# A Perceiver block on one core: convolution in token layout on GpSimd, bias row on VectorE, and some reordering

## The reference

```python
x = x + xattn(layernorm(x), ctx, ctx)     # q, k, v and output projections with biases, one head, softmax over 8192 keys
x = x + linear_attn(layernorm(x))         # 16 heads of 32: relu(rmsnorm(q)), relu(rmsnorm(k)); q (k^T v) / (q sum(k) + eps), W_out, b_out
x = x + ffn(layernorm(x))
# ffn, with h = layernorm(x), 8 experts, the 2 best by sigmoid(h Wr) + router_bias:
routed = sum over e < 4 of cw[e] * ((silu(h Wg[e]) * (h Wu[e])) Wd[e])
routed += cw[4] * h + cw[6] * h + cw[7] * relu(h)
shared = depthwise causal convolution of h over tokens, 4 taps, one weight per tap and channel, + conv_b
ffn = routed + shared
```

## Time and profile before

| | us |
|---|---|
| median of 3 runs | 531.51 |
| the profiled execution | 530.95 |
| its span, first to last instruction | 529.1 |
| TensorE busy | 524.3 |
| VectorE busy | 362.2 |
| ScalarE busy | 243.7 |
| GpSimd busy | 198.4 |

### The profile page before, as it was taken

The page is one execution under the profiler, slowest core; times in us unless marked ns, Lnnn a source line. Parts: engine busy times, 40 slices in busy tenths (PEclk is TensorE's granted clock), DMA queues, the critical chain, the costliest instruction groups (busy, mean ns, idle before and its releaser), DMA issues.

```text
span 529.1 us, 6966 instructions
## 1 busy us (share of the span) xinstructions
PE 524.3 (99%) x2542; PEld 436.5 (82%) x2542; DVE 362.2 (68%) x624; ACT 243.7 (46%) x392; POOL 198.4 (38%) x130
## 2 busy tenths in 40 slices
PE   9999999999999999999999999999999999999997
PEld 8888888888888888888888888888888878988886
DVE  5573666866668776556878554999967368548747
ACT  5743434745445454444535454657455332552210
POOL 3727050331211312233144442447439939900000
PEclk9999999999999999999999999999999999999999
DMA  8811222332422233422322211243330403300002
GB/s 297 321 60 61 80 97 102 111 129 81 159 81 79 81 118 123 157 82 81 141 96 80 81 56 65 79 160 119 119 121 1 159 2 123 117 1 0 2 0 79
DMA packets 15153, 51.60 MB, mean 98 GB/s; under 512 B 1808, under 2 KB 2320, under 8 KB 14480
## 3 DMA queue, kind: packets, MB, share of 16 engines
q1 hardware_dynamic: 14976, 51.03, 27.0%
q10 hardware_dynamic: 144, 0.13, 0.1%
HBM read 50.11 MB, written 1.05 MB: 97 GB/s over the span
## 4 chain that ended last, share of the span: by engine, by line
PE 97%; DVE 1%; ACT 1%; issue 0%; POOL 0%; POOLq 0%
PE bank L1405 27%; PE bank L1520 11%; PE bank L1531 11%; PE bank L1533 11%; PE bank L1521 11%; PE bank L1522 11%; PE bank L1532 11%; PE bank L1395 1%; PE bank L1452 1%; PE bank L1416 1%; PE bank L1668 1%; PE bank L1430 1%; DVE xT_l L911 0%; PE bank L1787 0%; ACT xn L651 0%; DVE stats L895 0%
## 5 line engine op out<-in xcount | busy, mean ns | idle before, releaser
L556 POOL TENSOR_TENSOR cn_l<-raw_n,cn_h 128x1024 fp32r<-128x1024 f32 x32 | 77.7, 2427 | 197.9 <-ACT cn_h L717 197.9
L735 ACT COPY ring<-bank 128x512 f32<-128x512 f32 x64 | 37.7, 589 | 148.3 <-PE bank L1522 148.0
L1030 DVE TENSOR_TENSOR top<-top,bank 128x512 f32<-128x512 f32 x60 | 41.1, 686 | 88.5 <-ACT ring L735 88.5
L1520 PE MATMUL bank<-qk_h,ct_h 128*128 128x512 f32 x256 | 99.6, 389 | 0.0
L1522 PE MATMUL bank<-qk_h,ct_l 128*128 128x512 f32 x256 | 99.6, 389 | 0.0
L1521 PE MATMUL bank<-qk_l,ct_h 128*128 128x512 f32 x256 | 99.6, 389 | 0.0
L1531 PE MATMUL bank<-ph,cn_h 128*128 128x512 f32 x256 | 99.6, 389 | 0.0
L1532 PE MATMUL bank<-pl,cn_h 128*128 128x512 f32 x256 | 99.6, 389 | 0.0
L1533 PE MATMUL bank<-ph,cn_l 128*128 128x512 f32 x256 | 99.6, 389 | 0.0
L1533 PEld LDWEIGHTS bank<-ph,cn_l 128*128 128x128 f32 x256 | 48.1, 188 | 10.1
L1522 PEld LDWEIGHTS bank<-qk_h,ct_l 128*128 128x128 f32 x256 | 48.1, 188 | 10.0
(11 more groups left out here) (248 smaller groups left out, 855.5 us busy)
## 6 DMA issues: line engine op xcount, KB each, us to landing
raw_t<-ctx_t SPq DMA_DIRECT2D x32, 512.0 KB, 4.2
raw_n<-ctx_n SPq DMA_DIRECT2D x32, 512.0 KB, 3.3
piece_raw<-pieces SPq DMA_DIRECT2D x12, 512.0 KB, 3.3
xs<-x SPq DMA_DIRECT2D x4, 256.0 KB, 5.5
wq_raw<-wq_t SPq DMA_DIRECT2D x4, 256.0 KB, 6.2
wk_raw<-wk_in SPq DMA_DIRECT2D x1, 1024.0 KB, 8.1
w_k_raw<-wqkv_in SPq DMA_DIRECT2D x1, 1024.0 KB, 7.4
w_out_raw<-wout_in SPq DMA_DIRECT2D x1, 1024.0 KB, 5.5
```

Source lines behind the costliest of these rows:

```text
L556: pool.tensor_tensor(cn[p % CNB][1][:], raw_n[p % 2][:], cn[p % CNB][0][:].bitcast(F32), ALU.subtract).then_inc(cnl_ready, 1)
L1030: dve.tensor_tensor(top[:], top[:], bank[:, S_BANKS[i % 2], :], ALU.max).then_inc(max_done, 1)
L1520: pe.matmul(bank[:, dst, :], ct[i // 2 % 2][0][:, c, keys], qk[0][:, c, :], start=(c == 0), stop=False)
```

## The change

- Bias row. The two products on TensorE, the split of `bv_wo` and `ones_r` go. VectorE sums `bv_wo` over partitions itself: `sum_bias` (at tile 9: transposition, sum), `gather_bias` (at 11: three small copies, a sum, four small copies), `spread_bias` (at 13: transposition, addition of `bo`).
- Head. The first half of `wo` is cast by VectorE, as its first instruction. VectorE's `first_stats(3)` moves ahead of `low_xT(0)`, ScalarE's `std_of(3)` ahead of `high_xT(1)`.
- Heads. TensorE makes `linear(2)` for chunks 0 and 1 only, then transposes the first tile's heads, chunks 0 and 1 as soon as VectorE's first half is there, then the rest of `linear(2)`. The z product of each tile is written as two halves; for tile 3 `transpose_x2(1)` stands between them.
- Convolution. `xf`, `whole_xT`, VectorE's four instructions for each chunk and TensorE's transposes go. The normalised tiles are written to DRAM (`xn_rows`, with three rows of zeros ahead) and loaded back three times, 1, 2 and 3 rows shifted, into two buffers `shifted`; taps and bias are loaded as rows broadcast to all partitions (`taps`, behind piece 8). GpSimd, after its last split, makes each tile with eight instructions of 128x512. Tile 1 waits for the router's weights.
- VectorE adds convolution tiles 0 to 2 in m = 6 and tile 3 behind `low_hid(7)`; expert 2 is added ahead of `low_hid(7)`.

```diff
+                if n == 8:
+                    sp.wait_ge(kv_psum, C)
+                    sp.dma_start(taps[:], taps_in.partition_broadcast(P)).then_inc(taps_loaded, 16)
+                if n == 10:
+                    sp.wait_ge(pads_ready, 2)
+                    sp.dma_start(xn_rows[0:PAD, :], tap_term[0:PAD, :]).then_inc(rows_written, 16)
+                    write_rows(0)
+            sp.wait_ge(rows_written, 16 * 2)
+            for t in range(TT):
+                b = t % 2
+                if t == 1:
+                    for n in range(1, TT):
+                        write_rows(n)
+                    sp.wait_ge(rows_written, 16 * (TT + 1))
+                    sp.wait_ge(g_psum, IC)
+                if t >= 2:
+                    sp.wait_ge(conv_ready, t - 1)
+                for j in range(1, TAPS):
+                    at_row = PAD + t * P - j
+                    sp.dma_start(shifted[b][:, j - 1, :], xn_rows[at_row:at_row + P, :]).then_inc(shift_loaded[b], 16)
...
+            pool.wait_ge(taps_loaded, 16)
+            for t in range(TT):
+                pool.wait_ge(xn_ready, 2 * TT + t + 1)
+                if t == 1:
+                    pool.wait_ge(cw_ready, 1)
+                conv_chain(pool.tensor_tensor(conv[:, t, :], xn[:, t, :], taps[:, PAD, :], ALU.mult))
+                conv_chain(pool.tensor_tensor(conv[:, t, :], conv[:, t, :], taps[:, TAPS, :], ALU.add))
+                pool.wait_ge(shift_loaded[t % 2], 16 * PAD * (t // 2 + 1))
+                for j in range(1, TAPS):
+                    conv_chain(pool.tensor_tensor(tap_term[:], shifted[t % 2][:, j - 1, :], taps[:, PAD - j, :], ALU.mult))
+                    ins = pool.tensor_tensor(conv[:, t, :], conv[:, t, :], tap_term[:], ALU.add)
+                    if j < PAD:
+                        conv_chain(ins)
+                ins.then_inc(conv_ready, 1)
...
+            dve.wait_ge(wo0_loaded[0], 16)
+            dve.tensor_copy(wo[0][:, 0, 0:HALF], wo_raw[:, 0, 0:HALF]).then_inc(wo0_ready, 1)
...
+            first_stats(3)
             low_xT(0, XT_BANKS)
-            first_stats(3)
...
+                if m == M - 2:
+                    for t in range(TT - 1):
+                        add_conv(t)
+            add_expert(EM - 2)
             low_hid(M - 1)
-            add_expert(EM - 2)
-            for t in range(TT):
-                dve.wait_ge(conv_psum, t + 1)
-                add_term(t, bank[:, t, :], None)
+            add_conv(TT - 1)
...
-                    pe.matmul(bank[:, BV_BANK, :], some, bv_parts[0][:], start=True, stop=False)
-                    pe.matmul(bank[:, BV_BANK, :], some, bv_parts[1][:], start=False, stop=True).then_inc(bv_psum, 1)
...
             transpose_heads(0)
+            linear(2, (2, 3))
             linear(TT - 1)
...
-            for t in range(TT):
-                for c in range(C):
-                    ins = pe.transpose(bank[:, t, c * P:(c + 1) * P], conv[:, c, t * P:(t + 1) * P], ident[:])
-                ins.then_inc(conv_psum, 1)
             down(M - 2)
             down(M - 1)
```

More of the change, by code:

```diff
@@ L368, in perceiver_block @@
         down_psum = sem("down_psum")
-        conv_psum = sem("conv_psum")
+        taps_loaded = sem("taps_loaded")
+        rows_written = sem("rows_written")
+        shift_loaded = [sem(f"shift_loaded{b}") for b in range(2)]
         out_ready = sem("out_ready")
@@ L692, in _ @@
             apply_of(2)
+            std_of(3)
             high_xT(1, XT_BANKS)
-            std_of(3)
             apply_of(3)
@@ L1661, in _, with linear @@
                         ins.then_inc(kv_psum, 1)
-            def linear(t):
+            def linear(t, chunks=range(C)):
                 pe.wait_ge(qrT_ready, C)
-                for c in range(C):
+                for c in chunks:
                     if t == 0:
@@ L1669, in linear @@
                                     qrT[:, c, t * P:(t + 1) * P], kv[:, c, :], start=True, stop=True)
-                ins.then_inc(la_psum, 1)
-            for t in range(TT - 1):
-                linear(t)
-            def transpose_heads(t):
-                pe.wait_ge(heads_ready, t + 1)
-                transpose_tile(heads, t, HEAD_BANKS[t]).then_inc(xnT_psum, 1)
+                if c == C - 1:
+                    ins.then_inc(la_psum, 1)
+            linear(0)
+            linear(1)
+            linear(2, (0, 1))
+            def transpose_heads(t):
+                if t > 0:
+                    pe.wait_ge(heads_ready, t + 2)
+                    transpose_tile(heads, t, HEAD_BANKS[t]).then_inc(xnT_psum, 1)
+                    return
+                for c in range(C):
+                    if c % 2 == 0:
+                        pe.wait_ge(heads_ready, c // 2 + 1)
+                    ins = pe.transpose(bank[:, HEAD_BANKS[0], c * P:(c + 1) * P], heads[:, 0, c * P:(c + 1) * P], ident[:])
+                ins.then_inc(xnT_psum, 1)
             def transpose_x2(t):
@@ L1692, in _ @@
                     transpose_x2(0)
-                    transpose_x2(1)
-                project(HEAD_BANKS[t], [cut(xT, c, t * P, (t + 1) * P) for c in range(C)],
-                        [cut(wout, c, 0, D) for c in range(C)]).then_inc(z_psum, 1)
+                for half in ((0, 1), (2, 3)):
+                    if t == TT - 1 and half[0] > 0:
+                        transpose_x2(1)
+                    ins = project(HEAD_BANKS[t], [cut(xT, c, t * P, (t + 1) * P) for c in half],
+                                  [cut(wout, c, 0, D) for c in half], starts=(half[0] == 0), stops=(half[0] > 0))
+                ins.then_inc(z_psum, 1)
                 if t < 2:
```

128 lines of the change are left out of this document (60 added, 68 removed).

## The result

| | before | after |
|---|---|---|
| median (5 runs each, same chip), us | 531.39 | 529.25 |
| lowest to highest | 531.10 to 532.03 | 528.48 to 529.44 |
| the profiled execution | 530.95 | 529.33 |
| its span | 529.1 | 527.2 |

The ratio is 0.9963, with an interval of 0.9951 to 0.9974: 1.4 to 2.6 us faster, 2.0 by the ratio. The forecast was 528.9, between 528.0 and 530.3. The span lost 1.93 us where 2.5 were forecast, and the whole profiled execution only 1.62.

What follows compares the result with a forecast made beforehand. TensorE, busy 524.3 of 529.1 us, was taken as the bound. 1.75 + 0.46 + 0.30 + 0 + 0.31 + 0 - 0.3 = 2.5 us gain, giving 528.9 us; own range 528.2 to 529.6, widened to 528.0 to 530.3.

Steps and rivals of the forecast that it cites:

- transposes off TensorE: Between `down(5)` and `down(6)`: the 16 `conv` transposes leave TensorE's stream with nothing in their place, gain 1.75 us.
- stall ahead of `down(6)`: At the end, `low_hid(6)` waits for GpSimd, delaying expert 2's additions; with `low_hid(7)`, loss 0.3 us, between 0 and 1.
- bias row: Cross attention: two TensorE products go, gain 0.46 us; VectorE's new steps at tiles 9, 11 and 13 cost TensorE nothing.
- fourth statistics: In the head, VectorE's statistics of the fourth x tile ahead of `low_xT(0)` bring its transposes sooner, gain 0.30 us.
- first cast: At the start, casting on VectorE brings between 0 and 0.1 us, taken as 0, since the fourth tile's transposes hold TensorE.
- heads: Ahead of the first z product, half of `linear(2)` behind the first head transposes closes a hole, gain 0.31 us (0 to 0.32).
- z split: At the last z product, products between transposes hide a 0.22 us wait; between -0.1 and +0.12 us, taken as 0.
- The router: Near 475 us, its small instructions meet GpSimd's last two of tile 0; weights, ready after 476.36 before, come by 478.4.
- The rule on two inputs from SBUF: Trainium skill: VectorE instructions with two SBUF inputs and GpSimd ones reading SBUF exclude each other; without it, gain 2.8 us, 528.6.
- A: Rival: GpSimd still works at 520.5, `low_hid(6)` and `low_hid(7)` both wait 1.3 us; 529.9 to 530.7 us, chance 0.17.
- B: Rival: GpSimd's convolution ends last, after 524.2 us, delaying the final additions; slower, 535.5 us, chance 0.05.
- C: Rival: `down(6)` waits for other reasons, so removing the transposes brings nothing; 1.1 us gain remains, 530.4 us, chance 0.07.

Runs made afterwards that it cites:

- E1: Changed kernel with GpSimd's last convolution tap of token tile 3 left out (two instructions fewer); median 528.58 us, ratio to the kernel before 0.9957.
- E5: Changed kernel with the bias row made as before (two TensorE products, split on GpSimd); median 528.92 us, ratio to the kernel before 0.9966.
- E7: Changed kernel with the fourth x tile's statistics behind `low_xT(0)` again and heads and `linear(2)` in one piece; median 529.58 us, ratio to before 0.9976.
- E6: Changed kernel with the first cast back on ScalarE and the z product in one piece; median 529.28 us, ratio to the kernel before 0.9975.
- E9: Changed kernel with buffers moved and the taps loaded behind piece 1 instead of piece 8; median 528.87 us, ratio to the kernel before 0.9961.
- E2: Changed kernel with the last tap product of token tile 3 made three times (two more GpSimd instructions); median 529.40 us, ratio to before 0.9972.
- E12: The changed kernel timed again, unedited, on the chip of the last group of runs; median 529.73 us, ratio to the kernel before 0.9976.
- E3: Changed kernel with `key_terms` split, its small copies and last sum moved behind tile 8's maximum; median 529.19 us, ratio to the kernel before 0.9968.
- E4: Changed kernel with the taps loaded ahead of piece 6 instead of behind piece 8; median 530.66 us, ratio to the kernel before 0.9998.
- E8: Changed kernel with the edits of E3 and E4 together; median 530.53 us, ratio to the kernel before 0.9998.
- E10: Changed kernel with `high_hid(6)` and `low_hid(6)` moved earlier and convolution tile 2 added at the very end; median 528.92 us, ratio to before 0.9962.
- E11: Changed kernel with the edits of E3, E9 and E10 together; median 528.82 us, ratio to the kernel before 0.9961.

## Why the prediction held, step by step

| term | forecast | measured | by |
|---|---|---|---|
| transposes off TensorE | 1.75 | 1.72 | before less E1 |
| stall ahead of `down(6)` | -0.3 (0 to -1) | -0.69 | after less E1 |
| bias row | 0.46 | 0.10 | E5 |
| fourth statistics | 0.30 | 0.30 + 0.16 scatter of the head | both profiles, E7 |
| first cast | 0 | 0 | E6 |
| heads | 0.31 | 0.34 | E7 |
| z split | 0 | 0.01 | E6 |
| stretch ahead of `linear` | 0 | -0.03 | before less after |
| sum, in the span | 2.5 | 1.93 | |
| around the span | 0 | -0.3 | time less span |
| sum, profiled execution | 2.5 | 1.62 | |

The number came out well within the range, but not every step did, and part of the agreement is luck: 0.16 us of the gain is scatter of the head, and the kernel timed again gained 1.3 us by the ratio, not 2.0. The two ends of the forecast's own range don't have the same base: 528.2 is 3.0 below the middle of both times before (531.23), 529.6 is 1.3 below the profiled execution (530.95). From the middle the range ended at 529.9.

*Convolution.* The mechanism was right in each part, and the term of the stall was the mis-sized one. GpSimd's end came at 516.86, within "between 514 and 518"; but two errors partly cancelled on the way. The router was hit harder than I counted: not two of its instructions but three, each standing for a whole GpSimd instruction, so the weights came 3.2 us later than before (478.65 and 0.90 that this execution is ahead, against 476.36) and not 2. Each of the 16 meetings then cost GpSimd 0.33 us (1.62 less 1.29) instead of 0.45, and the 24 instructions took 37.9 us instead of 40.3. The 0.45 was read rightly: two of the four GpSimd instructions of the earlier trace rows took 1.74 us where the others took 1.28. Those weren't chained; the convolution's are, and there it was less. Why is not shown. The stall follows from where in a GpSimd instruction `low_hid(6)` falls. Its length in seven executions is 0.68 (E1), 1.10 (E7), 1.18 (E9), 1.33 (E6), 1.74 (after), 1.76 (E2), 1.78 (E12), and the experts' stretch less 63.65 is 0, 0.05, 0.13, 0.28, 0.69, 0.73, 0.75. Above 1.05 us of length each tenth costs TensorE a tenth. The slack is thus 0.37 us, where I had 0.5, and the changed kernel met near its longest wait both times it was profiled, where I took the mean wait. Over eight executions (those above without E1, with E3 at 0.45 and E5 at 0.24, 0.05 of which lies elsewhere in the stage; E4 and E8 left out) the mean stall is 0.42. The rule on two inputs from SBUF that the prediction weighed holds in every row from 464 us on. A VectorE instruction with two operands in SBUF waits for a GpSimd one that began before it (`low_hid(6)`, 1.74 us). One with an operand in PSUM doesn't: `hid_full` takes 0.69 us at 515.07 beside GpSimd and 0.69 before, and four additions take 2.71 beside it in E2 and 2.72 in E1, where it has ended.

*Bias row.* Here a step failed: "that block costs TensorE nothing now, and the new ones come at the same load". It cost nothing because the two products that go were its cover: they put TensorE 0.46 us behind VectorE's maximum of tile 8. No hole stands at the new blocks at tiles 9, 11 and 13; it is the old one at tile 7 that turned into a hole. The hole and its slow first product are 0.24 of the 0.36 us missed. E3, which moves 0.8 us of VectorE's work out of the way, brings back 0.32. The rest goes in the small steps, 0.15 us of them between 90 and 95 us; E3 has 0.10 of these too when held against E5. What makes them stays open.

*Head.* The order was worth what was forecast; the other 0.16 us is that this execution's chain of statistics ran 0.17 sooner already at the third tile (11.66 against 11.83). In E3, E10 and E11 the same code came later there than before (12.96, 12.52, 12.42).

*Heads, z, first cast* came as worked out. The taps made pieces 9 and 11 late by 1.60 and 0.34 us and no one else waited, as said, yet E4 shows that this was a narrow place: the same load three pieces sooner takes the gain of the median.

*The rivals.* A (two waits at the end) did not come, and not even with two instructions more; half of A's stall did, within the forecast's own range. B needs GpSimd to end after 524.2 by the kernel before's clock; it ended at 517.8 by that, over six us sooner. C is excluded by the 1.03 us between gates and `down(6)`.

## What to carry to other kernels

Before an instruction is taken off the bounding engine, look at what has its slack only because of it: a neighbour that "costs nothing now" may be covered by the very work that goes. When work moves to GpSimd beside a busy VectorE, its price, here, is up to one GpSimd instruction of waiting ahead of each VectorE instruction with two operands in SBUF, so those with a deadline are better kept out of its reach by order (E10) than by speed. A load slipped into a queue is worth trying at more than one place: three pieces sooner took the gain here, at the front it showed no cost. And compare time less span between kernels: 0.3 us sat there that no row within the span shows.

## What was not expected of the hardware

- The longest wait of a VectorE instruction is the same whatever its length, about 1.1 us: instructions of 0.21 us took up to 1.31, those of 0.68 up to 1.78. GpSimd pays 0.33 us beside those of 512 columns (1.62 instead of 1.29), but at most 0.09 beside the router's small ones in this trace.
- Where VectorE has several such instructions in a row, it and GpSimd take turns: three additions in 5.18 us, 1.7 each, in step with GpSimd's starts 1.70 apart (508.77, 510.47, 512.17).
- The head of nearly the same code scatters more than any small term here: the queries started between 18.00 and 19.34 us in the executions with the new order. Counted from the third statistics it is 6.38 in eleven of them and 6.46 in one, so all of the scatter comes earlier, from data that land late (E3's row above) or from casts that came late (in E10 VectorE sat 1.94 us for a cast of `wv` at 6.97). Medians of a few runs move by tenths of a us with it; the same kernel, timed twice, gave ratios of 0.9963 and 0.9976.
- What lies around the span is a property of the kernel: 1.74 to 1.88 us in every execution of the kernel before, E2 and E5, 1.93 to 2.14 in every one of the others.
